# Second attention: GpSimd's work on whole rows waits for the parts of minus the maximum, maxima run ten heads ahead, and their rows go ahead of the loads

## The chip, the cores and the metric

One kernel runs on one core of a Trainium2 chip. The metric is the time of one execution on the device, in microseconds (us); several executions are timed and the median is given. The engines are TensorE (PE, with its weight loads as PEld), VectorE (DVE), ScalarE (ACT), GpSimd (POOL) and SyncE (SP), which here issues every transfer. Each engine runs its own instructions in order, and they meet at semaphores.

## The reference

The input is `x` (32 batches of 112 rows of 256) and a context (32 batches of 375 rows of 256). Four stages follow one another, each added to x:

```python
x = x + L0_xattn(layernorm(x), ctx)          # one head of 256, softmax over 375 rows
x = x + L0_ffn(layernorm(x))                 # three blocks: linear, layernorm, gelu, linear, residual
x = x + L1_xattn(ctx, layernorm(x))          # 16 heads of 16, softmax over 375 rows, output projection
x = x + L1_ffn(layernorm(x))                 # rmsnorm, ternary weights, 8-bit rounded activations, squared relu
```

The change is in the third, the second attention. For each batch and head it computes

```python
attn = softmax(q @ k.T * 16 ** -0.5)         # 112 x 375 for each of 16 heads
out  = (attn @ v) @ w_out.T + b_out          # 112 x 256 for a batch
```

and the last stage then needs the normed rows of the new x.

## The kernel before, in words

The second attention takes the 32 batches one after the other. Queries and keys were written to DRAM as three bfloat16 parts each, in earlier stages, and are brought back as tiles `qs` and `ks`, three buffers of each, so a batch's loads reuse the buffers of three batches before (`load_half`, L503: six transfers for heads 0 to 7, six for 8 to 15, some 730 KB a half).

Each head's scores are computed twice. The first time (`scores_for_max`, L1714) TensorE makes 112 x 375 scores of one head in one of three PSUM banks, and VectorE takes minus the maximum of each row (`maxima`, L1268) into a column of `nm`; the bank is free after that. When all 16 columns of a batch are there, VectorE splits them into three bfloat16 parts with four small instructions on 112 x 16 values (`parts_m`, L1272 to L1281: cast, subtract, cast, subtract). TensorE turns the parts (`turn_m`, L1727), ScalarE copies them to `mrow` (`m_out`, L953), and SP sends them into three rows of the batch's `qs` (`rows_m`, L517). The second time (`scores`, L1731) the three rows ride along in the product, so the scores come out with the maximum already taken off, turned with the context along the partitions, four heads and a third of the context at a time: 12 slots u = 0 to 11 a batch. ScalarE takes exponentials (`exps`, L939), TensorE weighs the values (`weigh`, L1744; pairs of slots, at u = 4, 6, 8, 10, 12, 14), and the sums of the batch are finished during the next batch: `fin_rows`, `fin_turn`, `fin_project` on TensorE (L1759 to L1776), `norm_o` (L1283), `x4` (L1291), `stats4`, `aggregate4`, `keep4` (L1297 to L1309) on VectorE.

The order of each engine is written out by hand, in `step3`. TensorE's step of batch b (L1778) has 15 slots; in slots 0 to 11 it makes the shifted scores of b, and in each slot (and once behind them) the scores for the maximum of one head of a later batch. Those run AHEAD = 7 heads ahead: the step of b takes heads 7 to 15 of b+1, then 0 to 6 of b+2. The head 15 of b+1 falls into slot 8, and `turn_m`(b+1) stands at the end of slot 10 (g, c = 3, 1). VectorE's step (L1311) goes through the same 16 maxima as positions k = 0 to 15, with `norm_o` behind k = 1, `x4` behind 5, `parts_m` behind 8, `stats4`, `aggregate4` and `keep4` behind 10, 11 and 12. ScalarE's `m_out` stands behind slot 10's exponentials.

SP's order for batch b is `moves` (L565): wait for slot 5's scores and load half 0 of b+3, send the rows of b+1, wait for slot 11's scores and load half 1 of b+3, store y of b-2 and x of b-1.

GpSimd's order for a batch (L791): `lay_v`(b+3) (L725) lays out the values of b+3, once batch b's have been weighed, and adds the output bias to its row of x; `factors4`(b) (L733) makes the row factors of the last stage's norms with eight small instructions, once `keep4`(b) has made the statistics; `norm_y`(b) (L755) turns the x row of b into the normed row y with three instructions on 112 x 256 values, once the row of x is stored.

Of the kernel before, what the change touches and what calls it, by code (L numbers as in the profile page):

```python
# [17 lines left out]
def xattn_ffn_kernel(  # L18
# [5 lines left out]
    B, L, D = x.shape  # L24
# [3 lines left out]
    TP = T // TC  # L28
    H, DH = 16, D // 16
    H8 = P // DH  # L30
    AHEAD = 7
    HQ = H // 4
    VW = DH + 1
    NLIN = L0_ffn_qweights.shape[0]
# [23 lines left out]
    with ExitStack() as ctx:  # L58
# [228 lines left out]
        passed_pool, passed_dve, passed_sp = sems("passed_pool passed_dve passed_sp")  # L287
# [70 lines left out]
        def apart(eng, passed):  # L358


            eng.sem_inc(passed, 1)
# [48 lines left out]
        def _(sp):  # L410
# [106 lines left out]
            def rows_m(b, par):  # L517
                sp.wait_ge(ones_rows_made, b + 1 if isinstance(b, int) and b < 3 else 3)
                sp.wait_ge(minus_max_rows_ready, b + 1)
                sp.dma_start(qs[par][KS:KS + 3, 0:H * L].rearrange("p (h l) -> p h l", h=H),  # L520
                             mrow[0:3 * H, :]).then_inc(minus_max_in_place, 16)
# [43 lines left out]
            def moves(b, par):  # L565

                more = not isinstance(b, int) or b < B - 3
                if more:
                    sp.wait_ge(shifted_scores_made, 12 * b + 6)
                    load_half(b + 3, par, 0)  # L570
                if not isinstance(b, int) or b < B - 1:
                    rows_m(b + 1, (par + 1) % 3)
                if more:
                    sp.wait_ge(shifted_scores_made, 12 * b + 12)
                    load_half(b + 3, par, 1)
                if not isinstance(b, int) or b >= 2:
                    store_y(b - 2)
                if not isinstance(b, int) or b >= 1:
                    store_x(b - 1)
                if isinstance(b, int) and b >= B - 3:  # L580
                    load_y(b - (B - 3), b - 1)
                if isinstance(b, int) and b == B - 2:
                    sp.wait_ge(ffn2_weights_in, 16)
                    everywhere_late(n2_bc, L1_ffn_norm2_w, HID)
                    sp.dma_start(w1T4.rearrange("p k n -> p (k n)"), wd[0]).then_inc(ffn2_weights_in, 16)
                    sp.dma_start(w2T4.rearrange("p c n -> p (c n)"), wd[1]).then_inc(ffn2_weights_in, 16)
# [31 lines left out]
        def _(pool):  # L618
# [106 lines left out]
            def lay_v(b, par, n):  # L725
                if not isinstance(b, int) or b >= 3:
                    pool.wait_ge(values_weighed, 12 * (b - 2))
                pool.tensor_copy(vaug[par][:, :, 0:H * VW].rearrange("p c (h w) -> p c h w", w=VW)[:, :, :, 0:DH],
                                 v_view[0:TP, row(b), :].rearrange("p o (c h w) -> p (o c) h w", c=TC, w=DH)
                                 ).then_inc(v_laid_out, 1)  # L730
                x_row = xs[:, row(b), :].rearrange("p o d -> p (o d)")
                pool.tensor_tensor(x_row, x_row, bout_bc[0:L, :], ALU.add).then_inc(x_plus_bout_made, 1)
# [22 lines left out]
            def norm_y(b):  # L755

                x_row = xs[:, row(b), :].rearrange("p o d -> p (o d)")
                pool.wait_ge(x_stored, 16 * (b + 1))
                apart(pool, passed_pool)
                pool.tensor_tensor(x_row, x_row, rs4[:, row(b)].broadcast_to([L, D]), ALU.mult).then_inc(ffn2_row_factor_steps, 1)  # L760
                pool.wait_ge(ffn2_row_factor_steps, 10 * b + 9)
                apart(pool, passed_pool)
                pool.tensor_tensor(x_row, x_row, rr4[:, row(b)].broadcast_to([L, D]), ALU.subtract).then_inc(ffn2_row_factor_steps, 1)
                pool.wait_ge(ffn2_row_factor_steps, 10 * b + 10)
                apart(pool, passed_pool)
                pool.tensor_tensor(x_row, x_row, n1_bc[0:L, :], ALU.mult).then_inc(y_made, 1)
# [21 lines left out]
                pool.memset(vaug[b][:, :, 0:H * VW].rearrange("p c (h w) -> p c h w", w=VW)[:, :, :, DH:VW], 1.0)  # L788
                lay_v(b, b, 0)
            pool.wait_ge(ffn2_weights_in, 16)  # L790
            with pool.Fori(0, (B - 3) // 3) as i:  # L791
                for m in range(3):
                    lay_v(3 * i + 3 + m, m, i)
                    factors4(3 * i + m)
                    norm_y(3 * i + m)
            for b in range(B - B % 3, B):
                lay_v(b, b % 3, 0)
            for b in range((B - 3) // 3 * 3, B):
                factors4(b)
                norm_y(b)  # L800

# [23 lines left out]
        def _(act):  # L825
# [131 lines left out]
            def step3(b, par, n):  # L957
                if not isinstance(b, int) or b >= 1:
                    pv_out(b - 1)
                for u in range(12):  # L960
                    exps(b, u)
                    if u == 3 and (not isinstance(b, int) or b >= 1):
                        o_out(b - 1)
                    if u == 10 and (not isinstance(b, int) or b < B - 1):
                        m_out(b + 1)
            def xq_out(i, par):

# [53 lines left out]
        def _(dve):  # L1021
# [289 lines left out]
            def step3(b, par, n):  # L1311
# [3 lines left out]
                for k in range(H):  # L1315
                    if k < H - AHEAD:
                        if not isinstance(b, int) or b < B - 1:
# [149 lines left out]
        def _(pe):  # L1467
# [310 lines left out]
            def step3(b, par, n):  # L1778


                later = not isinstance(b, int) or b >= 1
                heads = [(b + 1, (par + 1) % 3, n + (par == 2), h) for h in range(AHEAD, H)]
                if isinstance(b, int) and b == B - 1:
                    heads = []
                if not isinstance(b, int) or b < B - 2:
                    heads += [(b + 2, (par + 2) % 3, n + (par >= 1), h) for h in range(AHEAD)]
                for g in range(HQ + 1):
                    for c in range(TC):
                        if g < HQ:
                            scores(b, par, g, c)  # L1790
                        if heads:
                            scores_for_max(*heads.pop(0))
                        u = TC * g + c
                        if u >= 4 and u % 2 == 0:
                            weigh(b, par, (u - 4) // TC, (u - 4) % TC)
                            weigh(b, par, (u - 3) // TC, (u - 3) % TC)
                        if later and (g, c) == (0, 1):
                            fin_rows(b - 1)
                        if later and (g, c) == (1, 0):
                            fin_turn(b - 1)  # L1800
                        if later and (g, c) == (1, 2):
                            fin_project(b - 1)
                        if (g, c) == (3, 1) and (not isinstance(b, int) or b < B - 1):
                            turn_m(b + 1)
                if heads:
                    scores_for_max(*heads.pop(0))
# [88 lines left out]
```

## Time and profile before

| | |
|---|---|
| three runs, median (lowest to highest) | 1326.2 us (1320.96 to 1332.5) |
| the profiled execution's own time | 1329.82 us |
| its span, first to last instruction | 1328.0 us, mean granted TensorE clock 0.927 |
| busy in the span | PE 1113.8 (84%), PEld 783.1 (59%), DVE 917.8 (69%), ACT 539.3 (41%), POOL 515.1 (39%) |
| chain that ended last, by engine | PE 52%, DVE 19%, ACT 8%, issue 8%, SP's queue 5%, DMA 4%, POOL 2% |
| maxima, L1270 (VectorE) | 512 instructions, 257.8 us, mean 539 ns; idle before them 47.1 us |
| scores for the maximum, L1724 (TensorE) | 512 matmuls, 170.7 us, mean 347 ns |
| shifted scores, L1740 (TensorE) | 1536 matmuls, 143.8 us |
| values weighed, L1754 (TensorE) | 3072 matmuls, 116.5 us |
| `factors4` of one batch (GpSimd) | its eight instructions from 923.44 to 927.19 in the timeline |

Busy times are shares of the whole span and average over four stages with different limits; a stretch has to be read for itself. Neighbouring matmuls overlap, so TensorE's busy time counts some time twice. Spans on GpSimd are rough. Start times in the timelines are us from the span's first instruction.

### The profile page before, as it was taken

To read this page: it belongs to the slowest core of one execution; us is meant where nothing else is said; L and a number is where in the kernel's file an instruction comes from. 1 tells how busy PE (TensorE), PEld (TensorE's weight loads), DVE (VectorE), ACT (ScalarE), POOL (GpSimd) and SP (SyncE) were. 2 spreads that over 40 slices of the span, in tenths; PEclk is the share of its full clock that TensorE was granted. 3 is DMA by queue.
4 is the path that set the end of the run, shared out by engine and by line. 5 is a ranking of instruction groups with operands and counts; after the bars stand their busy time and mean duration, and the time that the engine had idled before them with its cause. 6 is when DMAs were issued, how large, how long until landed. Compare 5 with 4: busy or idle time off the path is not lost.

```text
span 1328.0 us, 30836 instructions
## 1 busy us (share of the span) xinstructions
PE 1113.8 (84%) x9234; PEld 783.1 (59%) x9234; DVE 917.8 (69%) x2318; ACT 539.3 (41%) x953; POOL 515.1 (39%) x875
## 2 busy tenths in 40 slices
PE   3699999999997889898864888988888889776675
PEld 2577777777775565665542465656565656534443
DVE  2646666666664575767564788888888888478886
ACT  1332322222222211111132355555555555568886
POOL 0324444444442122222103144444444444366664
PEclk7699999999998999999987799999999999868988
DMA  9323222233331000000027866666665666540000
GB/s 218 106 90 88 87 87 87 87 88 92 91 93 47 1 1 0 0 0 0 1 57 153 157 132 137 130 131 134 128 137 126 142 124 131 161 150 24 24 24 32
DMA packets 121314, 116.07 MB, mean 87 GB/s; under 512 B 45076, under 2 KB 114231, under 8 KB 121271
## 3 DMA queue, kind: packets, MB, share of 16 engines
q1 hardware_dynamic: 121270, 115.55, 36.4%
q8 instruction: 21, 0.34, 0.1%
q14 instruction: 23, 0.18, 0.1%
HBM read 79.15 MB, written 36.00 MB: 87 GB/s over the span
## 4 chain that ended last, share of the span: by engine, by line
PE 52%; DVE 19%; ACT 8%; issue 8%; SPq 5%; DMA 4%; POOL 2%; DVEq 1%; ACTq 0%; POOLq 0%
PE bank L1484 23%; PE bank L1642 6%; DVE nm L1270 5%; PE bank L1740 3%; PE bank L1578 3%; PE bank L1754 3%; PE bank L1724 3%; ACT v_all L995 2%; ACT v_all L988 2%; DVE npart L1279 2%; DVE hT L1189 2%; ACT v_all L982 2%; DMA qs<-mrow 2%; PE bank L1567 2%; DVE yn L1178 1%
## 5 line engine op out<-in xcount | busy, mean ns | idle before, releaser
L1270 DVE TENSOR_REDUCE nm<-bank 112x1 f32<-112x375 f32 x512 | 257.8, 539 | 47.1 <-PE bank L1724 44.3
L943 ACT ACTIVATE pT<-bank 125x448 f32<-125x448 f32 x384 | 192.2, 542 | 103.9 <-PE bank L1754 77.6
L1724 PE MATMUL bank<-ks,qs 96*128 96x375 bf16 x512 | 170.7, 347 | 21.5 <-DMA qs<-q_parts_dram 18.4
L1740 PE MATMUL bank<-qs,ks 128*128 128x112 bf16 x1536 | 143.8, 218 | 8.6 <-DMA qs<-mrow 7.8
L1740 PEld LDWEIGHTS bank<-qs,ks 128*128 128x128 bf16 x1536 | 104.2, 101 | 44.2 <-issue 29.5
L1754 PE MATMUL bank<-pT,vaug 125*32 125x112 f32 x3072 | 116.5, 270 | 0.0
L1642 PE MATMUL bank<-wffT,hT 128*112 128x256 f32 x384 | 100.7, 396 | 0.0
L894 ACT ACTIVATE yT<-bank,bcol,gcol 128x448 f32<-128x448 f32 x48 | 32.2, 721 | 163.4 <-PE bank L1624 163.4
L1754 PEld LDWEIGHTS bank<-pT,vaug 125*32 125x32 f32 x3072 | 68.8, 111 | 38.2 <-issue 34.1
L1484 PE MATMUL bank<-wv1T,ctxT 128*125 128x256 f32 x384 | 88.0, 379 | 0.0
L1484 PE MATMUL bank<-ctxT,wk1T 128*128 128x375 f32 x256 | 86.0, 478 | 0.0
L1169 DVE BATCH_NORM_STATS2 bs<-bank 112x6 f32<-112x256 f32 x96 | 36.6, 423 | 67.1 <-PE bank L1642 67.1
L807 POOL TENSOR_TENSOR v_all<-v_all 128x1024 f32<-128x1024 f32 x28 | 66.6, 2379 | 41.5 <-DVE v_all L1364 41.5
L1484 PEld LDWEIGHTS bank<-wv1T,ctxT 128*125 128x125 f32 x384 | 71.9, 187 | 17.2
L1724 PEld LDWEIGHTS bank<-ks,qs 96*128 96x128 bf16 x512 | 50.5, 100 | 53.3 <-issue 27.1
L704 POOL TENSOR_SCALAR ve<-mv 112x2 f32<-112x2 f32 x48 | 10.7, 222 | 171.7 <-DVE mv L1148 171.7
L1484 PE MATMUL bank<-yT,wffT 128*128 128x448 f32 x192 | 76.2, 540 | 0.1
L875 ACT ACTIVATE pr<-bank,ebias 112x375 f32<-112x375 f32 x32 | 18.4, 574 | 141.1 <-DVE ebias L1121 141.1
L1642 PEld LDWEIGHTS bank<-wffT,hT 128*112 128x112 f32 x384 | 65.2, 187 | 16.2 <-issue 1.8
L1624 PE MATMUL bank<-ident,yn 112*128 112x112 f32 x320 | 42.6, 281 | 38.1 <-DVE yn L1178 20.7
L1624 PEld LDWEIGHTS bank<-ident,yn 112*128 112x128 f32 x320 | 34.8, 151 | 58.1 <-DVE yn L1178 36.0
L1484 PEld LDWEIGHTS bank<-ctxT,wk1T 128*128 128x128 f32 x256 | 48.4, 189 | 32.9
(204 smaller groups left out, 2343.6 us busy)
## 6 DMA issues: line engine op xcount, KB each, us to landing
k_parts_dram<-kp SPq DMA_DIRECT2D x192, 93.8 KB, 3.5
ks<-k_parts_dram SPq DMA_DIRECT2D x64, 281.2 KB, 4.2
cnat<-in_ctx_dram SPq DMA_DIRECT2D x32, 375.0 KB
ks<-k_parts_dram SPq DMA_DIRECT2D x64, 187.5 KB, 3.9
ks<-k_parts_dram SPq DMA_DIRECT2D x64, 93.8 KB, 3.3
q_parts_dram<-qp SPq DMA_DIRECT2D x48, 112.0 KB, 2.2
qs<-q_parts_dram SPq DMA_DIRECT2D x64, 84.0 KB, 4.0
x_stream<-in_x_dram SPq DMA_DIRECT2D x4, 896.0 KB, 13.8
```

The lines of the kernel that those rows point to most:

```text
L807: pool.tensor_tensor(gh[par], th[par], n2_bc, ALU.mult).then_inc(hidden_weighted, 1)
L894: last = act.activation(yT[s][:, c, :], YT[s][:, c, :], ACT.Gelu, bias=bcol[:, k, c:c + 1], scale=gcol[:, k, c:c + 1])
L943: act.activation(pT[:, u % 4, :], B3[u % 3][0:TP], ACT.Exp).then_inc(probs_made, 1)
L1169: dve.bn_stats(bs2[s][:, t, :], LIN[s][:, t, :]).then_inc(lin_stats[s], 1)
L1270: dve.tensor_reduce(nm[:, h:h + 1], A3[h % 3][0:L], AX_X, ALU.max, negate=True).then_inc(head_max_taken, 1)
L1484: last = mm(o, lhs(k), rhs(k), start=(k == 0), stop=(k == KC - 1))
L1578: last = mm(AT1[:, k, :], cnat[par][:, c, k * P:(k + 1) * P], prT[:, c, :], start=(c == 0), stop=(c == TC - 1))
L1624: last = pe.transpose(YT[s][:, c, t * L:(t + 1) * L], yn[s][:, t, c * P:(c + 1) * P], ident[0:L, 0:L])
L1642: last = mm(LIN[s][:, t, :], hT[s][:, c, t * L:(t + 1) * L], wffT[:, 2 * k, c, :], start=False, stop=(c == KC - 1))
L1724: mm(A3[h % 3], qs[par][0:KS, h * L:h * L + P], ks[par][0:KS, h * T:(h + 1) * T], start=True, stop=True).then_inc(max_scores_made, 1)
L1740: last = mm(B3[c][:, j * L:(j + 1) * L], ks[par][:, h * T + c * TP:h * T + c * TP + P], qs[par][:, h * L:(h + 1) * L], start=True, stop=True)
L1754: last = mm(PV3[32 * j:32 * j + 32, g, :], vaug[par][:, c, h * VW:h * VW + 32], pT[:, u % 4, j * L:(j + 1) * L], start=(c == 0), stop=(c = ...
```

## The change

AHEAD becomes 10: the step of batch b takes the scores for the maximum of heads 10 to 15 of b+1 and 0 to 9 of b+2. `parts_m` follows by its formula (k = H - AHEAD - 1) from position 8 to 5, where `x4` stands just ahead of it. `turn_m` moves from the end of slot 10 to the end of slot 8, and ScalarE's `m_out` from behind slot 10's exponentials to behind slot 8's. On SP the rows of b+1 now come first, then half 0 of b+3, then half 1. On GpSimd the order of a batch becomes: wait until `parts_m` of b+2 is done, `norm_y`(b-1), `lay_v`(b+3), `factors4`(b); the last batches follow without that wait.

```diff
--- before.py
+++ after.py
@@ -28,7 +28,7 @@
     TP = T // TC
     H, DH = 16, D // 16
     H8 = P // DH
-    AHEAD = 7
+    AHEAD = 10
     HQ = H // 4
     VW = DH + 1
     NLIN = L0_ffn_qweights.shape[0]
@@ -565,11 +565,11 @@
             def moves(b, par):
 
                 more = not isinstance(b, int) or b < B - 3
+                if not isinstance(b, int) or b < B - 1:
+                    rows_m(b + 1, (par + 1) % 3)
                 if more:
                     sp.wait_ge(shifted_scores_made, 12 * b + 6)
                     load_half(b + 3, par, 0)
-                if not isinstance(b, int) or b < B - 1:
-                    rows_m(b + 1, (par + 1) % 3)
                 if more:
                     sp.wait_ge(shifted_scores_made, 12 * b + 12)
                     load_half(b + 3, par, 1)
@@ -788,14 +788,25 @@
                 pool.memset(vaug[b][:, :, 0:H * VW].rearrange("p c (h w) -> p c h w", w=VW)[:, :, :, DH:VW], 1.0)
                 lay_v(b, b, 0)
             pool.wait_ge(ffn2_weights_in, 16)
-            with pool.Fori(0, (B - 3) // 3) as i:
+
+
+
+            def rows3(b, par):
+                pool.wait_ge(minus_max_parts_made, b + 3)
+                apart(pool, passed_pool)
+                if not isinstance(b, int) or b >= 1:
+                    norm_y(b - 1)
+                lay_v(b + 3, par, 1)
+                factors4(b)
+            for b in range(3):
+                rows3(b, b)
+            with pool.Fori(1, (B - 3) // 3) as i:
                 for m in range(3):
-                    lay_v(3 * i + 3 + m, m, i)
-                    factors4(3 * i + m)
-                    norm_y(3 * i + m)
-            for b in range(B - B % 3, B):
-                lay_v(b, b % 3, 0)
-            for b in range((B - 3) // 3 * 3, B):
+                    rows3(3 * i + m, m)
+            for b in range((B - 3) // 3 * 3, B - 3):
+                rows3(b, b % 3)
+            norm_y(B - 4)
+            for b in range(B - 3, B):
                 factors4(b)
                 norm_y(b)
 
@@ -961,7 +972,7 @@
                     exps(b, u)
                     if u == 3 and (not isinstance(b, int) or b >= 1):
                         o_out(b - 1)
-                    if u == 10 and (not isinstance(b, int) or b < B - 1):
+                    if u == 8 and (not isinstance(b, int) or b < B - 1):
                         m_out(b + 1)
             def xq_out(i, par):
 
@@ -1800,7 +1811,7 @@
                             fin_turn(b - 1)
                         if later and (g, c) == (1, 2):
                             fin_project(b - 1)
-                        if (g, c) == (3, 1) and (not isinstance(b, int) or b < B - 1):
+                        if (g, c) == (2, 2) and (not isinstance(b, int) or b < B - 1):
                             turn_m(b + 1)
                 if heads:
                     scores_for_max(*heads.pop(0))
```

## Rows read from the trace of the kernel before

**Rows 1.** Busy us by stretch (PE, PEld, DVE, ACT, POOL), clock, DMA share, GB/s.

```profile
756.80:1133.00 376.20, 330.72 (x4964) 222.21 (x4963) 329.06 (x754) 205.57 (x435) 160.01 (x369) 0.96 0.62 131
925.35:938.50 13.15, 11.02 (x173) 7.41 (x171) 11.74 (x28) 7.09 (x15) 5.75 (x14) 1.00 0.63 131
1121.39:1133.02 11.63, 11.09 (x173) 7.33 (x171) 10.27 (x27) 6.96 (x15) 5.06 (x15) 1.00 0.31 77
```

**Rows 2.** Lines of VectorE: minimum/median/maximum ns, first and last start.

```profile
L1286 DVE RECIPROCAL rden<-bank x32: 245/249/259, 756.8 to 1152.2; 112x16 f32<-112x16 f32 x32
...
L1279 DVE CAST npart<-nres x32: 174/1359/1446, 737.9 to 1139.2; 112x16 bf16<-112x16 f32 x32
...
L1281 DVE TENSOR_TENSOR npart<-nres,npart x32: 174/653/657, 738.1 to 1139.5; 112x16 bf16<-112x16 f32 x32
...
L1270 DVE TENSOR_REDUCE nm<-bank x512: 508/539/550, 729.3 to 1138.3; 112x1 f32<-112x375 f32 x171
```

**Rows 3.** VectorE's timeline: start, us, instruction, [idle before, releaser].

```profile
925.35 0.25 DVE L1286 RECIPROCAL rden<-bank 112x16 f32<-112x16 f32 x1
...
927.90 0.55 DVE L1270 TENSOR_REDUCE nm<-bank 112x1 f32<-112x375 f32 x1 [0.44 <-PE bank L1724]
928.88 0.42 DVE L1295 TENSOR_TENSOR x_stream<-bank,x_stream 112x256 f32 x1 [0.43 <-PE bank L1484]
...
930.11 1.00 DVE L1270 TENSOR_REDUCE nm<-bank 112x1 f32<-112x375 f32 x2 [0.35 <-PE bank L1724]
931.15 0.38 DVE L1275 CAST npart<-nm 112x16 bf16<-112x16 f32 x1
...
933.84 0.99 DVE L1270 TENSOR_REDUCE nm<-bank 112x1 f32<-112x375 f32 x2
...
1127.19 0.17 DVE L1275 CAST npart<-nm 112x16 bf16<-112x16 f32 x1
...
1128.34 0.18 DVE L1281 TENSOR_TENSOR npart<-nres,npart 112x16 bf16<-112x16 f32 x1
```

**Rows 4.** GpSimd's timeline over the same parts.

```profile
930.09 0.61 POOL L760 TENSOR_TENSOR x_stream<-x_stream,rs  x1 [2.90 <-DMA x_rows_dram<-x_stream]
...
932.37 0.83 POOL L728 COPY vaug<-v_all 125x768 f32 x1
933.16 0.72 POOL L732 TENSOR_TENSOR x_stream<-x_stream,bout_bc 112x256 f32 x1
```

**Rows 5.** Waits from 756.8 to 1133: us, times, longest.

```profile
PE bank L1729 <- DVE npart L1281: 32.8, 27, 1.6
...
PE bank L1740 <- DMA qs<-mrow: 3.9, 16, 0.6
```

**Rows 6.** TensorE's timeline in the period from 925.35.

```profile
927.70 1.03 PE L1484 MATMUL bank<-woT,pvs 128*112 128x256 f32 x4
...
930.36 0.59 PE L1754 MATMUL bank<-pT,vaug 125*32 125x112 f32 x16
...
933.97 0.25 PE L1729 MATMUL bank<-identb,npart 112*96 112x112 bf16 x1 [1.58 <-DVE npart L1281]
```

**Rows 7.** SP's issues in the same period.

```profile
927.66 0.35 SPq L532 DMA_DIRECT2D x_rows_dram<-x_stream  x1
928.33 0.61 SPq L510 DMA_DIRECT2D ks<-k_parts_dram  x1
...
931.98 0.37 SPq L513 DMA_DIRECT2D qs<-q_parts_dram  x1
934.59 0.83 SPq L520 DMA_DIRECT2D qs<-mrow  x1
935.68 0.65 SPq L510 DMA_DIRECT2D ks<-k_parts_dram  x1
```

**Rows 8.** Transfers, median us to landing: from 756.8 to 1133, and from 724 to 756.

```profile
qs<-q_parts_dram SPq DMA_DIRECT2D x56, 28.0 KB, 3.2
...
qs<-q_parts_dram SPq DMA_DIRECT2D x7, 28.0 KB, 4.3
```

## The prediction

> **What bounds the kernel now.** Read first the busy times of stretches. The second attention's steady part lasts 376.2 us, 28% of the span, and neither TensorE (330.7 us, 88%) nor VectorE (329.1 us, 87%) is full in it; DMA is at 0.62, the granted clock at 0.96 [rows 1]. Its unit is one batch: from one `rden` reciprocal of VectorE (L1286) to the next. 32 of them start between 756.8 and 1152.2 [rows 2], and the first 29 gaps fill the 376.2 us, so a period is now 12.97 us on average. The period from 925.35, at full TensorE clock, is 13.15 us; one late in the stage, when few loads are left (DMA 0.31), is 11.63 [rows 1]. What differs?
>
> The medians of the instructions of `parts_m` answer it: each takes 0.17 us at its best, but the second cast's median is 1.36 us and the last subtraction's 0.65 us [rows 2]. VectorE's timeline shows where: from 931.15 four tiny instructions keep it until 933.84, 2.69 us [rows 3]. Over them, on GpSimd's timeline, lie `norm_y` (from 930.09), the value layout of `lay_v` (932.37 to 933.20) and the x row with its bias (933.16 to 933.88) [rows 4]. In the period of 11.63 us the same four, 1127.19 to 1128.52, take 1.33 us [rows 3]: 1.36 us less in the parts, 1.52 us less in the period. So the stretch is on the path nearly one for one.
>
> The table of waits says why. TensorE's turn of the parts (L1729) waits for them 32.8 us in this stretch, 27 times [rows 5]; at 933.97 it had waited 1.58 us [rows 6]. VectorE itself goes on with its maxima at 933.84, and the next reciprocal starts at 925.35 + 13.15 = 938.50: 4.66 us in which its timeline has no wait. The shifted scores are hardly held up by the rows of the maximum: 3.9 us in 16 waits [rows 5].
>
> **The change, part by part.** (a) *Ten heads ahead.* Maxima are neither added nor removed. The last one of the next batch falls at position 5 instead of 8, just before `x4`, which keeps its position; so `parts_m` comes right after `x4`. Build the new period from [rows 3]: reciprocal, `on`, three maxima and a wait 2.55 us (925.35 to 927.90); maximum 5 and the wait for the projection 0.98 (to 928.88); `x4` and maximum 6 0.88 (to 930.11, without the wait of 0.35 there); maxima 7 and 8 1.0. The parts undisturbed: four at 0.17 and their gaps, 0.75. Then 4.66 as before. The wait of 0.35 us goes, because the parts now stand in it. Sum 10.8 us.
>
> TensorE must follow. The turn moves to slot 8, behind the weighing at 930.36 [rows 6]. The projection, four matmuls from 927.70, was over at 928.6, so TensorE comes to the turn 2.4 us after it; VectorE has the parts 0.3 + 0.34 + 0.75 = 1.4 us after it. That wait goes whole; what is late next is maximum 6, whose bank slot 9 needs, by at most one maximum of 0.54. TensorE's own work: it is busy 11.09 of the 11.63 us [rows 1], with overlaps of neighbours counted twice, so its floor lies a little under 11. With two engines so close and three score banks between them I add 0.2 us of mutual waits.
>
> (b) *GpSimd's big pieces behind the parts.* `norm_y`(b-1) and `lay_v`(b+3) now start after the parts of b+2: five instructions, 930.09 to 933.88, 3.8 us. `norm_y` still needs the stored x row, and SP comes to that later now (below): some 13.2 us after the projection, landed 2.4 us on (927.66 to 930.09, [rows 4, 7]). So they run from 4.2 to 8 us after the next projection, and `factors4` (eight small ones, 3.8 us in the table ahead) to about 11.8, that is 0.4 us into the following one, where the parts begin. Its queue has nothing else behind it, and who waits for it (`weigh` of b+3, `x4` of b+3, the y store) wants it a period or more later. Two overlaps follow that no row shows. `keep4`'s copy, at about 5.0, meets `norm_y`: between 0 and the 1.2 us by which a cast was stretched; I take 0.3, since `norm_y`'s first is only 0.61 us long [rows 4]. The parts meet the last small ones: 0 to 0.5 us (a stretched last subtraction); I take 0.1. Alone, this edit would give the 1.4 to 1.9 us that stand between 0.75 and the stretched parts.
>
> By the rows, cast and subtraction between SBUF tiles stretch, and maxima, which read PSUM, stay at 508 to 550 ns [rows 2]. The Trainium skill, "SBUF — State Buffer", section "Who interferes with whom", says the same: casts and copies may lock the port pair that VectorE shares with GpSimd, for a whole instruction, two-SBUF-input instructions contend with GpSimd's reads, and reductions never do. By that rule `keep4`'s copy is fair game, which speaks against part of the gain; no row here shows that copy under such a load.
>
> (c) *Rows ahead of the loads.* SP's order becomes rows, half 0, half 1, y, x. From [rows 7]: rows to first load 1.09, each half 3.65 + 0.37, two stores at 0.67 to 0.8: 10.6 us of SP a period. Half 0 was issued behind slot 5; now it waits for the rows, issued 3.4 us after the projection (turn at 2.4, then ScalarE's exp and copy, then SP). Its last issue starts 1.09 + 3.65 later, at 8.1, and lands after 3.2 us [rows 8]: 11.3. It is needed at slot 6 instead of 9, a period + 0.2 after. So the loop of loads wants 11.1 us; with 4.3 us of landing, as at the stage's start with its full queue [rows 8], 12.2. Half 1 follows 4 us later and is needed, at slot 13, nearly 5 us later.
>
> (d) *The edges.* Three more maxima ahead of batch 0, 3 x 0.54 = 1.6 us; against them the first turn and its rows come three slots sooner and pass half a load on SP. Counted at nothing, with 2 us either way. The end's chain through x, y and the tiles keeps its order.
>
> **Sum.** Period: 10.8 + 0.2 + 0.3 + 0.1 = 11.4 us. 29 x (12.97 - 11.4) = 45.5 us less. The profiled execution took 1329.8 us (span 1328.0): 1284.3 for it. It lay 3.6 us over the median of the three runs, 1326.2, so against that: **1281 us**.
>
> **The rivals.** *A, transfers pace it.* For: SP at 10.6 and the loads at 11.1 are close under my period, and landings rise from 3.2 to 4.3 us when the queue is full. Against: only 0.62 of DMA is used now. Period 12.2: 29 x 0.77 = 22 less, 1304. *B, the collision moves* to `keep4`'s copy, 1.2 us instead of 0.3, which is what the skill's rule would make of it at worst: period 12.3 less the slack this opens elsewhere (0.2), 12.1, 25 less, 1301. *C, little happens:* the parts are quick, but something I took for slack carries the path, and the period ends at 12.6 or more: 1315 to 1326. Against it is the period of 11.63 us in the old order. *D, slower.* SP's loads stand behind the rows, and the rows behind both halves and both stores of the batch before. The place: TensorE's slot 6, waiting for half 0. It costs time against before once the last landing takes 5.1 us (8.1 + 5.1 = 13.0 + 0.2). At 5.7 us the period is 13.6, 18 us more: 1344. Against: 4.3 us is the landing even at the full queue, and SP issues each half no faster than today.
>
> **How the numbers follow.** Own forecast 0.62 (period 10.8 to 11.9: 1263 to 1295), A 0.16, B 0.08, C 0.09, D 0.05. The likeliest gives 1281. The range runs from 1264 (10.8 us) to 1305 (12.25 us), which takes in A and B and the edges, and leaves out C and D. A measurement of this kernel tells about 1% (13 us) from no change. Faster by over 1%: 0.62 + 0.16 + 0.08 = 0.86; within 1%: 0.09; slower: 0.05.
>
> **What would show it.** Medians of the four parts near 0.18 us, L1279 above all; the L1729 wait near nothing; reciprocals 11.4 us apart; the clock at 1.0 in the stage. L1309's copy shows B by its mean. A wait of L1724 for a load, once a period, and grown landings show A, or D above 13 us. I would be wrong if the parts are quick and the period still is over 12 with no such wait; then the 4.66 us after the parts hid something.

## The result and the profile after

The changed kernel takes 1276.2 us (median of 4, 1273.95 to 1277.96) against 1327.9 for the kernel before in the same comparison (median of 4): a ratio of 0.962, 95% interval 0.959 to 0.965. The profiled execution of it took 1277.96 us, span 1276.0. The forecast was 1281 and 1264 to 1305.

The stretches, as in [rows 1] (us; busy PE, PEld, DVE, ACT, POOL; clock, DMA share, GB/s):

```profile
754.50:1082.50 328.00, 309.77 (x4962) 210.17 (x4960) 286.67 (x755) 200.18 (x436) 157.42 (x364) 1.00 0.76 152
902.17:913.43 11.26, 10.67 (x175) 7.22 (x173) 9.81 (x27) 6.88 (x15) 5.61 (x14) 1.00 0.78 152
```

The first 29 periods now fill 328 us in place of 376.2: 11.31 us each instead of 12.97. VectorE's busy time in them fell by 42 us (329.1 to 286.7), TensorE's by 21 (330.7 to 309.8) for the same matmuls, with the clock granted in full, 1.00 for 0.96. TensorE is busy 94% of the stretch.

The 0.96 needs a look of its own. Two neighbouring periods of the kernel before, in the same columns:

```profile
1030.52:1043.36 12.84, 11.02 (x173) 7.42 (x171) 11.45 (x27) 7.08 (x15) 5.57 (x13) 1.00 0.65 135
1043.36:1057.31 13.95, 12.17 (x173) 8.07 (x171) 11.84 (x27) 7.18 (x15) 6.29 (x15) 0.88 0.66 136
```

In eight of the 29 periods before, the granted clock fell from 1.00 to 0.50 (1.2 GHz instead of 2.4) for a stretch, in the second of these two from 1052.85 to 1056.26. Where the parts lasted about 2.5 us, five such periods average 13.90 us and six at full clock 12.88. So a fall costs about 1.0 us, and by that estimate eight of them make 0.3 us of the average of 12.97, or 8 us of the time. Seven of the eight falls come within 2.2 us of a turn for which TensorE had waited 1.3 to 1.6 us; ten other turns waited as long and no fall followed.

The 29 periods, 376.2 us before and 328.1 after, make 48.1 of the 52.0 us of span. The rest is at the edges: the first reciprocal starts 2.3 us earlier, and the last two periods take 17.7 us instead of 19.2, since fewer maxima are left for the last steps.

The lines of VectorE, as in [rows 2] (minimum/median/maximum ns; all lines behind the edit on GpSimd are 11 further on: L1297 is the reciprocal, L1290 and L1292 the second cast and the last subtraction, L1320 `keep4`'s copy):

```profile
L1297 DVE RECIPROCAL rden<-bank x32: 235/246/258, 754.5 to 1100.3; 112x16 f32<-112x16 f32 x32
...
L1290 DVE CAST npart<-nres x32: 174/174/177, 737.0 to 1086.7; 112x16 bf16<-112x16 f32 x32
...
L1292 DVE TENSOR_TENSOR npart<-nres,npart x32: 174/175/208, 737.2 to 1086.9; 112x16 bf16<-112x16 f32 x32
...
L1320 DVE COPY mv<-mv x32: 156/160/1295, 763.1 to 1111.6; 112x2 f32 x27, 112x2 f32<-112x2 f32 x5
```

The cast fell from a median of 1359 ns to 174, the subtraction from 653 to 175, and neither ever took over 208. The copy's median stayed at 160 ns; nine of the 32 took from 254 to 1295.

VectorE's timeline of one period, which stands against [rows 3]:

```profile
902.17 0.25 DVE L1297 RECIPROCAL rden<-bank 112x16 f32<-112x16 f32 x1
...
904.73 0.55 DVE L1281 TENSOR_REDUCE nm<-bank 112x1 f32<-112x375 f32 x1 [0.44 <-PE bank L1735]
905.70 0.42 DVE L1306 TENSOR_TENSOR x_stream<-bank,x_stream 112x256 f32 x1 [0.43 <-PE bank L1495]
906.04 0.16 DVE L1286 CAST npart<-nm 112x16 bf16<-112x16 f32 x1
...
906.77 1.57 DVE L1281 TENSOR_REDUCE nm<-bank 112x1 f32<-112x375 f32 x3
908.76 1.00 DVE L1281 TENSOR_REDUCE nm<-bank 112x1 f32<-112x375 f32 x2 [0.42 <-PE bank L1735]
...
911.09 0.16 DVE L1320 COPY mv<-mv 112x2 f32 x1
911.16 2.36 DVE L1281 TENSOR_REDUCE nm<-bank 112x1 f32<-112x375 f32 x5
```

The parts follow on `x4` and last from 906.04 to 906.83, when the next maximum has begun. The maxima 6 to 8 begin at 906.77; a wait of 0.42 us now stands before maximum 9 (908.76), where TensorE brings the scores of slot 9 late. The copy (911.09) falls into the gap of 0.18 us between two pieces of `norm_y` (910.49 + 0.61 = 911.10, the next at 911.29). GpSimd in the same period, against [rows 4]:

```profile
910.49 0.61 POOL L760 TENSOR_TENSOR x_stream<-x_stream,rs  x1 [3.78 <-DMA x_rows_dram<-x_stream]
911.29 0.61 POOL L763 TENSOR_TENSOR x_stream<-x_stream,rr  x1 [0.18 <-POOL x_stream L760]
...
912.76 0.83 POOL L728 COPY vaug<-v_all 125x768 f32 x1
913.55 0.72 POOL L732 TENSOR_TENSOR x_stream<-x_stream,bout_bc 112x256 f32 x1
```

`norm_y` begins at 910.49, 3.7 us after the parts were done, and what it waited for is the stored row. TensorE and SP, against [rows 6] and [rows 7]:

```profile
904.52 1.03 PE L1495 MATMUL bank<-woT,pvs 128*112 128x256 f32 x4
...
905.99 0.33 PE L1735 MATMUL bank<-ks,qs 96*128 96x375 bf16 x1 [0.24 <-DMA qs<-q_parts_dram]
...
907.59 0.59 PE L1765 MATMUL bank<-pT,vaug 125*32 125x112 f32 x16
908.11 0.25 PE L1740 MATMUL bank<-identb,npart 112*96 112x112 bf16 x1
```

```profile
907.90 0.34 SPq L532 DMA_DIRECT2D x_rows_dram<-x_stream  x1
908.91 0.85 SPq L520 DMA_DIRECT2D qs<-mrow  x1
910.14 0.65 SPq L510 DMA_DIRECT2D ks<-k_parts_dram  x1
...
913.74 0.36 SPq L513 DMA_DIRECT2D qs<-q_parts_dram  x1
```

The turn (908.11) follows the weighing without a wait. But the score for the maximum in slot 6 (905.99) waits for half 0, whose last issue on SP starts 4.83 us after the rows' (908.91 to 913.74). The table of waits for the 29 periods, against [rows 5], and the landing of that last piece, against [rows 8]:

```profile
DVE nm L1281 <- PE bank L1735: 23.9, 59, 0.4
...
PE bank L1735 <- DMA qs<-q_parts_dram: 5.6, 14, 1.0
...
PEld bank L1735 <- DMA qs<-q_parts_dram: 1.2, 1, 1.2
```

```profile
qs<-q_parts_dram SPq DMA_DIRECT2D x57, 28.0 KB, 3.5
```

The 32.8 us of waiting for the parts are gone; 5.6 + 1.2 us of waiting for loads came, in 15 waits. In the chain of waits of one period (start, us, what) the rows, the first and last issues of half 0, its landing and the score in slot 6 follow on one another:

```profile
897.57 0.84 SPq L520
898.73 0.65 SPq L510
...
902.29 3.57 DMA qs<-q_parts_dram
905.99 0.33 PE bank L1735
```

### The profile page after: what moved, and what is told of

It reads as the page before. It is cut to its first block, busy times and chain, and to the rows that moved or that the text cites. A ratio compares the mean times of both kernels' runs of the same rounds, so it can differ in the third digit from the quotient of the medians.

```text
span 1276.0 us, 30834 instructions
## 1 busy us (share of the span) xinstructions
PE 1089.4 (85%) x9234; PEld 768.8 (60%) x9234; DVE 875.6 (69%) x2318; ACT 534.5 (42%) x953; POOL 515.3 (40%) x875
## 4 chain that ended last, share of the span: by engine, by line
PE 50%; DVE 12%; SPq 9%; issue 9%; ACT 8%; DMA 8%; POOL 2%; DVEq 1%; POOLq 0%; ACTq 0%
PE bank L1495 23%; PE bank L1653 6%; DMA qs<-q_parts_dram 5%; PE bank L1765 4%; PE bank L1589 3%; PE bank L1751 3%; SPq L510 3%; PE bank L1735 3%; ACT v_all L1006 3%; ACT v_all L999 2%; DVE nm L1281 2%; ACT v_all L993 2%; DVE hT L1200 2%; SPq L513 2%; PE bank L1578 2%
## 5 line engine op out<-in xcount | busy, mean ns | idle before, releaser
L1281 DVE TENSOR_REDUCE nm<-bank 112x1 f32<-112x375 f32 x512 | 254.0, 540 | 40.3 <-PE bank L1735 38.5
L1735 PE MATMUL bank<-ks,qs 96*128 96x375 bf16 x512 | 160.8, 337 | 25.5 <-DMA qs<-q_parts_dram 23.4
L1751 PE MATMUL bank<-qs,ks 128*128 128x112 bf16 x1536 | 139.7, 214 | 0.5 <-DMA qs<-mrow 0.5
L1751 PEld LDWEIGHTS bank<-qs,ks 128*128 128x128 bf16 x1536 | 104.7, 99 | 32.8 <-issue 17.1
L1765 PE MATMUL bank<-pT,vaug 125*32 125x112 f32 x3072 | 113.3, 265 | 0.0
L886 ACT ACTIVATE pr<-bank,ebias 112x375 f32<-112x375 f32 x32 | 18.4, 574 | 140.9 <-DVE ebias L1132 140.9
L1735 PEld LDWEIGHTS bank<-ks,qs 96*128 96x128 bf16 x512 | 46.6, 98 | 48.8 <-issue 32.3
```

The lines of the kernel that those rows point to most:

```text
L1281: dve.tensor_reduce(nm[:, h:h + 1], A3[h % 3][0:L], AX_X, ALU.max, negate=True).then_inc(head_max_taken, 1)
L1735: mm(A3[h % 3], qs[par][0:KS, h * L:h * L + P], ks[par][0:KS, h * T:(h + 1) * T], start=True, stop=True).then_inc(max_scores_made, 1)
L1751: last = mm(B3[c][:, j * L:(j + 1) * L], ks[par][:, h * T + c * TP:h * T + c * TP + P], qs[par][:, h * L:(h + 1) * L], start=True, stop=True)
L1765: last = mm(PV3[32 * j:32 * j + 32, g, :], vaug[par][:, c, h * VW:h * VW + 32], pT[:, u % 4, j * L:(j + 1) * L], start=(c == 0), stop=(c = ...
```

## The experiments

All carry the same kernel before; ratios are to it as it ran beside each. The period is the mean of the first 29 gaps between reciprocals, "parts" runs from the first cast's start to the last subtraction's end, a mean of the same 29.

| kernel | time, us | ratio (95%) | period | parts |
|---|---|---|---|---|
| before | 1326 to 1331 | 1 | 12.97 | 2.31 |
| changed | 1276.2 | 0.962 (0.959 to 0.965) | 11.31 | 0.80 |
| e1 GpSimd's wait only | 1308.2 | 0.986 (0.982 to 0.989) | 12.28 | 0.80 |
| e2 ten ahead only | 1270.5 | 0.958 (0.953 to 0.962) | 11.17 | 1.36 |
| e3 rows first only | 1287.4 | 0.970 (0.966 to 0.974) | 11.65 | 0.80 |
| e4 changed, no wait on GpSimd | 1275.7 | 0.960 (0.957 to 0.964) | 11.23 | 0.80 |
| e5 changed, old SP order | 1272.8 | 0.960 (0.957 to 0.963) | 11.11 | 0.79 |
| e6 before, narrow GpSimd work | 1286.7 | 0.969 (0.965 to 0.972) | 11.70 | 0.82 |
| e7 e1 with keep4 as a reduction | 1291.0 | 0.973 (0.970 to 0.977) | 11.65 | 0.80 |
| e8 e2 with a later finish | 1272.8 | 0.958 (0.954 to 0.961) | 11.11 | 0.80 |
| e9 changed, half the keys loaded | 1266.8 | 0.951 (0.948 to 0.955) | 10.96 | 0.80 |
| e10 e5 with keep4 as a reduction | 1268.4 | 0.952 (0.949 to 0.955) | 11.00 | 0.79 |
| e11 e10 with half the projection | 1266.9 | 0.951 (0.947 to 0.954) | 10.99 | 0.79 |
| e12 changed, again beside e9 to e11 | 1276.8 | 0.958 (0.955 to 0.961) | 11.25 | 0.80 |

### The three edits one at a time, and the change without the wait

**e1.** GpSimd's new order and wait, the rest as before.

```diff
+            def rows3(b, par):
+                pool.wait_ge(minus_max_parts_made, b + 3)
...
+                    norm_y(b - 1)
+                lay_v(b + 3, par, 1)
+                factors4(b)
...
```

Expected: 

> The kernel before with one edit: GpSimd's norm_y and lay_v wait for the parts (maxima stay seven ahead, rows stay behind half 0). Theory 1 (the collision of GpSimd's whole-row work with VectorE's four small instructions is what the change takes away): the four fall to 0.8 us a batch, the period from 12.97 to 11.3 to 11.6 us, the time to 1277 to 1287 us, the granted clock of the stage rises to 1.0. Theory 2 (maxima ten heads ahead are the lever: they take the parts and the turn off the path): here the time stays over 1305 us, since the turn still stands right behind the parts.

The parts fell to 0.80 us and the clock rose to 1.00, but the period only to 12.28: 1308.2 us, 21 over the upper end. VectorE's timeline and GpSimd's show where the rest stayed:

```profile
907.53 0.17 DVE L1292 TENSOR_TENSOR npart<-nres,npart 112x16 bf16<-112x16 f32 x1
...
909.87 1.47 DVE L1320 COPY mv<-mv 112x2 f32 x1
911.26 2.35 DVE L1281 TENSOR_REDUCE nm<-bank 112x1 f32<-112x375 f32 x5
```

```profile
908.16 0.61 POOL L760 TENSOR_TENSOR x_stream<-x_stream,rs  x1 [4.87 <-DVE npart L1292]
...
909.83 0.73 POOL L766 TENSOR_TENSOR x_stream<-x_stream,n_bc 112x256 f32 x1 [0.19 <-POOL x_stream L763]
910.50 0.82 POOL L728 COPY vaug<-v_all 125x768 f32 x1
```

`keep4`'s copy of two values a row begins at 909.87 and ends at 911.34, with the layout of the values, which had begun at 910.50 right behind the 0.73 us piece before it. It takes 1.47 us here, 1376 ns in the median, instead of 0.16. The wait let GpSimd's big pieces start 0.46 us after the parts (907.70 to 908.16), and the collision moved on by one customer. And a second wait came up that was small before (16 times, 3.9 us in [rows 5]):

```profile
PE bank L1751 <- DMA qs<-mrow: 18.3, 29, 0.7
```

TensorE waits for the rows of the maximum once in each of the 29 periods, 18.3 us in all.

**e2.** Ten heads ahead alone (AHEAD, the turn, ScalarE's copy).

```diff
-    AHEAD = 7
+    AHEAD = 10
...
-                    if u == 10 and (not isinstance(b, int) or b < B - 1):
+                    if u == 8 and (not isinstance(b, int) or b < B - 1):
                         m_out(b + 1)
...
-                        if (g, c) == (3, 1) and (not isinstance(b, int) or b < B - 1):
+                        if (g, c) == (2, 2) and (not isinstance(b, int) or b < B - 1):
                             turn_m(b + 1)
```

Expected: 

> The kernel before with one edit: maxima ten heads ahead, with the turn behind slot 8 and ScalarE's copy behind slot 8's exponentials; GpSimd and SP in the old order. Theory 1: SP stores x some 8.3 us after the rows, which puts norm_y at 0.5 us before to 3.3 us after the projection, right over the parts (0.5 to 1.4 us after it), so the parts stay stretched at 2 us or more and the period is 12.0 to 12.5 us, of which the hidden wait has taken a part: 1299 to 1314 us. Theory 2: 1276 to 1285 us.

1270.5 us: below both, and the whole of the change's gain from one of its edits. The parts are still disturbed, though the move has taken them out of most of the collision: they last 1.36 us a batch in place of 2.31, where 0.80 is undisturbed. The subtractions are at medians of 322 and 548 ns:

```profile
L1277 DVE TENSOR_TENSOR nres<-nm,npart x32: 174/322/637, 734.1 to 1082.8; 112x16 f32<-112x16 f32 x32
...
L1281 DVE TENSOR_TENSOR npart<-nres,npart x32: 174/548/661, 734.5 to 1083.2; 112x16 bf16<-112x16 f32 x32
```

What is left of the stretch costs less than its length, because the parts stand where VectorE had been waiting for TensorE. Its waits for scores and the waits for the rows:

```profile
DVE nm L1270 <- PE bank L1724: 13.7, 31, 0.6
...
PE bank L1740 <- DMA qs<-mrow: 0.9, 2, 0.7
```

VectorE waits 13.7 us for scores here and 23.9 in the changed kernel. The rows come early enough by now. So theory 1 as I had it, stretch equals lost time, fell here. But the rest of the stretch is not free. The nearest kernel without any is e10 below, which has the same order on SP: there VectorE is busy 10.3 us less over the 29 periods (283.4 for 293.7) and the periods last 5.0 us less in all (319.0 for 324.0), so about half of the stretch lay in idle time. By the medians of the periods, 11.22 here and 10.89 there, it costs more than by the means. How much of e2's gain comes from the smaller collision, how much from the place of the rest and how much from the earlier turn is not shown.

**e3.** SP sends the rows ahead of half 0; nothing else.

```diff
+                if not isinstance(b, int) or b < B - 1:
+                    rows_m(b + 1, (par + 1) % 3)
                 if more:
                     sp.wait_ge(shifted_scores_made, 12 * b + 6)
                     load_half(b + 3, par, 0)
-                if not isinstance(b, int) or b < B - 1:
-                    rows_m(b + 1, (par + 1) % 3)
```

Expected: 

> The kernel before with one edit: SP sends the rows ahead of half 0. Theory 1: the stores of x come some 4 us later on SP, so norm_y and lay_v move off the parts by themselves; the four fall below 1.2 us a batch and the time to 1277 to 1292 us, though no wait is added. Theory 3 (the order on SP matters only for the rows, whose wait was 3.9 us in all): within 4 us of 1328, the parts still stretched.

1287.4 us, within theory 1. The order on SP moves the collision away without a word about it on GpSimd: `norm_y` waits for the stored row until the parts are done, by 2.4 us in one period (908.79 to 911.23). The period stops at 11.65 with TensorE waiting for the rows in every one:

```profile
POOL x_stream L760 <- DMA x_rows_dram<-x_stream: 119.4, 28, 7.7
...
PE bank L1740 <- DMA qs<-mrow: 18.7, 29, 0.9
```

**e4.** The changed kernel with GpSimd's old loop, which is the same order without the wait.

```diff
-            def rows3(b, par):
-                pool.wait_ge(minus_max_parts_made, b + 3)
...
                 for m in range(3):
-                    rows3(3 * i + m, m)
...
+                    lay_v(3 * i + 3 + m, m, i)
+                    factors4(3 * i + m)
+                    norm_y(3 * i + m)
...
```

Expected: 

> The changed kernel without GpSimd's wait (its old order, which is the same but for the wait). Theory 1, with the timing read from the changed kernel's trace (x rows land 4.8 us after the parts): the wait never ends last, so the time is that of the changed kernel, 1274 to 1280 us. A rival that the wait itself is needed in the full change: parts stretched again, 1300 us or more.

1275.7 us, period 11.23: as the changed kernel. In the full change the wait never ends last; it is worth nothing there.

### What the collision costs, and where it can go

**e6.** The kernel before, with GpSimd's wide pieces made narrow. It leaves out most values of the normed rows, of the bias on the rows, and of the laid-out values from batch 3 on.

```diff
+                    dst, src = dst[:, 0:1, 0:1], src[:, 0:1, 0:1]
...
-                pool.tensor_tensor(x_row, x_row, bout_bc[0:L, :], ALU.add).then_inc(x_plus_bout_made, 1)
+                pool.tensor_tensor(x_row[:, 0:16], x_row[:, 0:16], bout_bc[0:L, 0:16], ALU.add).then_inc(x_plus_bout_made, 1)
...
+                x_row = x_row[:, 0:16]
...
-                pool.tensor_tensor(x_row, x_row, n1_bc[0:L, :], ALU.mult).then_inc(y_made, 1)
+                pool.tensor_tensor(x_row, x_row, n1_bc[0:L, 0:16], ALU.mult).then_inc(y_made, 1)
```

Expected: 

> The kernel before, where norm_y, the bias on the x row and lay_v (from batch 3 on) work on 16 columns or one piece instead of the whole row; all instructions, waits and transfers stay. It leaves out most of these values. Theory 1 (the width of GpSimd's work over the parts is the cost): the four near 0.8 to 1.1 us, period 11.6 us as with the rows first (then the rows' way through the turn bounds, 0.65 us of wait a period), 1282 to 1292 us. Theory 3 (the parts are slow for another reason, such as the transfers in flight): over 1315 us, parts still over 2 us.

1286.7 us. With order, waits and transfers untouched, the second cast is back at 175 ns:

```profile
L1282 DVE CAST npart<-nres x32: 174/175/234, 735.9 to 1099.8; 112x16 bf16<-112x16 f32 x32
```

The period is 11.70, within 0.05 of e3. The width of GpSimd's work cost the kernel before 1.3 us a batch. About 0.3 of it goes with the clock, which is granted in full in every period here, and 1.0 with the path. With seven heads ahead e3, e6 and e7 all end at 11.65 to 11.70, each with TensorE waiting for the rows in all 29 periods (18.7, 19.8 and 18.4 us), which says that the rows are the next bound.

**e7.** e1, with `keep4`'s copy written as a maximum over one element, which gives the same values.

```diff
-                dve.tensor_copy(mv4[:, row(b), :].rearrange("p o d -> p (o d)"), mv3[:, :]).then_inc(ffn2_row_stats, 1)
+                dve.tensor_reduce(mv4[:, row(b), :].rearrange("p o d -> p (o d)"), mv3[:, :].unsqueeze(2), AX_X, ALU.max).then_inc(ffn2_row_stats, 1)
```

Expected: 

> The kernel with GpSimd's wait alone, and keep4's copy written as a reduction over one element (same values). Theory 1 (in that run the stretch moved from the parts to this copy, 1.38 us instead of 0.16, on VectorE's path; a reduction is not stretched): the reduction takes under 0.25 us, the period falls from 12.28 to about 11.65 us, where the wait for the rows bounds, the time from 1308 to 1286 to 1292 us. Rival (the copy's stretch was in slack, the longer period came from the rows' wait): 1303 us or more.

1291.0 us, 17 less than e1 by one instruction a batch. It takes 145 ns, 155 at most, at the place where the copy took 1376:

```profile
L1320 DVE TENSOR_REDUCE mv<-mv x32: 142/145/155, 763.7 to 1118.1; 112x2 f32 x27, 112x2 f32<-112x2 f32 x5
```

It still runs under the same work of GpSimd, as one period shows:

```profile
903.40 0.14 DVE L1320 TENSOR_REDUCE mv<-mv 112x2 f32 x1
```

```profile
903.36 0.72 POOL L766 TENSOR_TENSOR x_stream<-x_stream,n_bc 112x256 f32 x1 [0.19 <-POOL x_stream L763]
```

The Trainium skill, "SBUF — State Buffer", section "Who interferes with whom", says that copies can contend with GpSimd for the shared port pair and that on this chip reductions never do. The trace agrees: 1376 ns against 145 for the same values.

### What bounds the changed kernel

**e5.** The changed kernel with SP's old order (half 0, rows, half 1).

Expected: 

> The changed kernel with SP's old order (half 0 ahead of the rows): ten heads ahead and GpSimd's wait. Theory 1, as the runs so far leave it (with ten heads ahead the parts stand in slack, TensorE's own work bounds, and the loads behind the rows cost the change 0.1 to 0.2 us a period at slot 6): no TensorE wait for qs or ks loads, period 11.1 to 11.2 us, 1268 to 1273 us, some 5 us under the changed kernel. Theory 2 (GpSimd's wait puts norm_y and lay_v onto keep4's copy, as it did alone): copy's median over 0.6 us and the time 1276 us or more.

1272.8 us, period 11.11: the waits for loads are gone. By the ratios it can't be told from the changed kernel (0.960 and 0.962, the intervals overlap); by the trace the rows' place ahead of half 0 costs 0.14 to 0.2 us a period with ten heads ahead (11.11 against 11.25 and 11.31). The copy is partly hit, a median of 376 ns:

```profile
L1320 DVE COPY mv<-mv x32: 156/376/528, 761.0 to 1101.6; 112x2 f32 x27, 112x2 f32<-112x2 f32 x5
```

**e8.** e2 with the finish of a batch one slot later, `x4` behind the parts. The turn also waits for `x4`, since the two share a bank.

```diff
-                    if u == 3 and (not isinstance(b, int) or b >= 1):
+                    if u == 4 and (not isinstance(b, int) or b >= 1):
                         o_out(b - 1)
...
-                    if later and k == 5:
+                    if later and k == 6:
                         x4(b - 1)
...
+                if not isinstance(b, int) or b >= 2:
+                    pe.wait_ge(x_after_attn2, b - 1)
...
-                        if later and (g, c) == (1, 0):
+                        if later and (g, c) == (1, 1):
                             fin_turn(b - 1)
-                        if later and (g, c) == (1, 2):
+                        if later and (g, c) == (2, 0):
                             fin_project(b - 1)
```

Expected: 

> The kernel before with ten heads ahead only, and the finish of a batch one slot later: fin_turn behind slot 4, fin_project behind slot 6, ScalarE's copy behind slot 4's exponentials, x4 behind the parts (the turn waits for x4 too, since they share a bank). If TensorE's wait for VectorE's on (0.37 us busy-free a period and 0.6 at its weight loads) bounds with its own work, the period falls from 11.17 to 10.8 to 11.0 us: 1260 to 1266 us. If that wait only moves to another place (the projection for ScalarE's copy, or maxima later), 1268 to 1276 us.

1272.8 us, no better than e2, although the parts, now ahead of `x4`, are undisturbed (0.80). TensorE's wait for `on` has gone, and another has come: VectorE now waits twice as long for the projection (22.5 us for 12.1), and TensorE for maxima.

```profile
DVE x_stream L1295 <- PE bank L1484: 22.5, 29, 0.8
...
PE bank L1724 <- DVE nm L1270: 13.2, 29, 0.5
```

**e9.** The changed kernel, with half the keys in each load from batch 3 on (the other heads keep an earlier batch's keys).

```diff
+                    cols = H8 * T // cut
-                    sp.dma_start(ks[par][at_row:at_row + n, half * H8 * T:(half + 1) * H8 * T],
-                                 one.unsqueeze(1).broadcast_to([DH, reps, H8 * T])).then_inc(half_in[half][par], 16)
+                    sp.dma_start(ks[par][at_row:at_row + n, half * H8 * T:half * H8 * T + cols],
+                                 one[:, 0:cols].unsqueeze(1).broadcast_to([DH, reps, cols])).then_inc(half_in[half][par], 16)
...
-                    load_half(b + 3, par, 0)
+                    load_half(b + 3, par, 0, cut=2)
...
-                    load_half(b + 3, par, 1)
+                    load_half(b + 3, par, 1, cut=2)
```

Expected: 

> The changed kernel, where from batch 3 on each load of keys brings the first four of a half's eight heads only (the issues, their number and order stay; the other heads keep old keys). Theory 1 (half 0, issued behind the rows, arrives late at slot 6 and sets the changed kernel's period at 11.3): landings shrink, TensorE's waits for qs and ks go, the period falls to 10.9 to 11.1 us, 1266 to 1271 us. If SP's issue time and not the transfer is the limit, or the loads are hidden: 1274 us or more.

1266.8 us, period 10.96. SP's issues are as many and in the same order, only the transfers are shorter; the last piece of a half lands after 1.8 us instead of 3.5:

```profile
qs<-q_parts_dram SPq DMA_DIRECT2D x56, 28.0 KB, 1.8
```

TensorE's waits for loads are gone. So shorter transfers are enough to free slot 6, without touching SP's issue time, and that is worth 0.29 to 0.35 us a period (11.25 in e12 beside it, 11.31 in the first profile). The issue time stands in the same chain; e5, which only moves the start of the issues, takes the waits away too.

**e10.** e5 and e7's reduction together: ten heads ahead, GpSimd's wait, SP's old order. Expected: 

> Ten heads ahead and GpSimd's wait, SP's old order, and keep4's copy as a reduction. Theory 1: this takes away both late loads and the copy's stretch of 0.22 us; what is left is TensorE's own work with its wait for on, the shortest periods seen (10.86): period 10.9 to 11.0, 1264 to 1270 us. If the copy's stretch lay in slack with ten heads ahead: 11.1 us and 1269 to 1275 us.

1268.4 us, 0.952 (0.949 to 0.955), where the changed kernel beside it had 0.958 (0.955 to 0.961): 0.6% faster by these ratios, and the lowest ratio of those that compute all. From e2's (0.953 to 0.962) the intervals don't part it. Most periods are 10.85 to 10.97, the median is 10.89; the mean is 11.00 us, with TensorE busy 97% of the stretch (308.9 of 319.0).

**e11.** e10 with one of the two products of the output projection left out.

```diff
-                over_rows(O3, lambda k: oT[:, k, :], lambda k: woT[:, k, :])
+                mm(O3, oT[:, 0, :], woT[:, 0, :], start=True, stop=True)
```

Expected: 

> The same with one of the two products of the output projection left out (0.43 us of TensorE a batch). If TensorE's path bounds the period, it falls by 0.4 to 0.45 us, 12 us of time, against the kernel with both; if VectorE or transfers bound, by under 0.15 us a period.

The period stays at 10.99. The shortest ones did fall, from 10.85 to 10.60, but TensorE's wait for the rows rose from 2.7 us (6 times) to 9.2 (21 times), and VectorE waits more for scores (15.4 us in e10):

```profile
DVE nm L1281 <- PE bank L1735: 29.8, 78, 1.5
...
PE bank L1751 <- DMA qs<-mrow: 9.2, 21, 1.5
```

So TensorE's work is one of several bounds close to one another, and taking from it alone gives nothing.

**e12.** The changed kernel again, beside e9 to e11. Expected: 

> The changed kernel as it is, beside the others on one chip: 1274 to 1280 us, some 8 to 10 us over the kernel with ten heads ahead, GpSimd's wait, the old order on SP and the reduction.

1276.8 us, as before. What separates e10 from it is 8.4 us.

## Why the prediction was right, step by step

**The bound before** was read rightly: stretched parts on the path. e6 shows it by itself (1287 us with nothing but GpSimd's width changed). "Nearly one for one" is right for long parts: among the periods before at full clock, six with parts of 1.99 us on average last 12.38 and five with parts of 2.68 last 13.08. It ends where the rows hold the period, at 11.64 with parts of 1.33 us and still at 11.65 with 0.80. So taking away 1.5 us of stretch (e6) gives 1.3 us of period, 1.0 on the path and about 0.3 by the clock. I had called the rows hardly a bound, from 3.9 us of waiting; the stretch had covered them, since it made each batch longer by more than the rows' way was late. My sum set the average of 12.97, with its stretches of low clock, against a period built at full clock; so it had the clock's 0.3 us in it without a word on them.

**(a) Ten heads ahead.** The built sum of 10.8 us holds: 10.85 is the shortest period of the changed kernel, and e10's usual one lies close to it. The turn's wait went whole. VectorE's second wait for scores, which I let go, is back in the changed kernel (0.42 us before maximum 9) and is all but gone in e10, where no load is waited for. What I missed is the rank of this part: it was one term of my sum, and alone it gives the whole gain (e2). It ends the rows' hold, it takes 0.95 of the 1.51 us of stretch away by moving the parts, and about half of the rest falls into VectorE's idle time.

**(b) GpSimd's wait.** I gave it 1.4 to 1.9 us alone; e1 measured 0.69. The step that failed is "alone, this edit would give": it left out the copy, which I had priced only for the full change, and the rows, which hold the period at 11.65 even with the copy unstretched (e7: 1.32 us). Rival B's mechanism is real, with 1.2 us as its price, in e1, where the big pieces start right behind the parts; in the full change the store it waits for lets `norm_y` begin only 3.7 us after the parts, so the copy, with 0.3 us allowed, cost 0.11 on average (268 ns for 157). That is partly luck: in the period shown the copy falls right into a gap between two pieces of `norm_y`, and in nine of the 32 batches it was hit, up to 1295 ns. There the wait is worth nothing (e4), and e5, which has it, is no faster than e2, which has not; with the copy as a reduction as well (e10) the period is 0.17 us under e2's. The 0.1 us for the parts among the last small instructions of `factors4` was nothing: those lie over the parts in the period shown, and no part took over 208 ns.

**(c) Rows ahead of the loads.** The loop of loads was put at 11.1 us and in the sum at nothing, because it stayed under 11.4. But it lay over the 10.8 on which the sum was built, so it should have been the bound there. It is what holds the changed kernel: 11.31 with it, 10.96 without (e9), 11.11 with the old order (e5). Its mechanism, slot 6 waiting for half 0, is that of rivals A and D; the landing rose from 3.2 to 3.5 us, not to 4.3 or 5.1. Alone the edit is worth 40 us (e3), again by moving the store and so `norm_y`, which I had worked out as a shift but not as a gain.

**The sum.** 11.4 against 11.31: the total is right and its composition partly is not. Of the 0.6 us over 10.8 I gave 0.4 to the copy and the last small instructions of `factors4`, which cost 0.11, and 0.2 to mutual waits; e9 puts 0.3 to 0.35 of the real 0.5 on the loads. Two errors of 0.3 us in opposite directions offset one another, which is luck. The edges gave 3.9 us where I counted none with 2 either way.

**Open.** Single long periods, such as the second of the changed kernel (13.04 us) and the 28th of several kernels (11.9 to 13.5), were not tried. Two such periods of e10, 11.66 and 12.49 us, make 0.08 of the 0.15 us between 10.85 and its mean of 11.00; what sets the rest is open, and e11 shows TensorE, VectorE's scores and the rows all close by. That the long waits at the turn bring the falls of the clock fits the runs, which lose both together, but was not tried by itself.

## What to carry to other kernels

Before pricing a stretched instruction, ask whether the stretch lies in a wait of its engine; moving the parts three positions was worth 57 us, though 0.56 us of stretch a batch stayed (e2); taking the stretch away in place was worth 39 (e6). When work is pushed off a victim by a wait, list the next instructions of the same kind that it will now meet (here a copy of two values), or write them in a form that doesn't contend. An order on a transfer queue can decide what two compute engines do to each other, since it dates the transfer that starts one of them.

## What the runs showed of the hardware

A VectorE copy of 112 x 2 values beside GpSimd's wide work took 1376 ns in the median and up to 1478, longer than any one GpSimd instruction over it (0.82): it ends with the second of two that follow one another without a gap, though not with the third, which follows as closely. It isn't always so: in the kernel before a first cast that began at 801.32, under the same two pieces, took 743 ns and ended with the first of them. What decides it is open. The same values by a reduction took 145 ns, and `x4`, which reads PSUM and one SBUF operand, 423 to 426 in the kernels before and after. The granted clock was 0.96 over the 29 periods before, by eight falls to 0.50, and 1.00 in every kernel whose period was 12.28 us or less.
